# Cross-attention and routed FFN on one core: where the scatters wait, and how the last layer norm is shared between engines

## The chip, the cores and the metric

One core of a Trainium2 chip runs the whole program. The metric is the device time of one execution in microseconds (us). Three runs of the kernel before took 785.79, 787.87 and 788.98 us; the median is 787.87 us.

## The reference, cut to what matters

```python
x = x + attention(_layernorm(x), ctx)              # x: 4096 tokens x 256, 32 tiles of 128 tokens
# FFN on h = _layernorm(x):
scores = softmax(h @ wg)                           # 8 experts
gates, idx = top_k(scores, 2)                      # each token goes to two experts
disp[e] = rows of h sent to expert e               # room for 1280 rows per expert
y[e] = silu(disp[e] @ fc1[e].T + b1[e]) @ fc2[e] + b2[e]
res = h + sum over the token's two experts of gate * y
ffn = (res - mean(res)) * rsqrt(var(res) + 1e-5) * gamma + beta
out = x + ffn
```

The part "h + sum of gate * y" and everything behind it is what the change touches. A token appears once in the rows of one expert and can appear again in those of another.

## The kernel before, in words

The program has three stages. Attention and the router run first, token tile by token tile; they leave `x` after attention in the SBUF tile `X` and store each normalised row twice in HBM: in `xn_rows`, from which the experts gather, and in `sum_rows`, in which the result `res` is built.

**Expert stage.** Eight experts have room for 1280 rows each, cut into five steps of 256 rows (`SPE` = 5), so there are 40 steps `st` of two halves (`NST` = 40). TensorE does fc1 of step c and fc2 of step c-1 (line 1082); steps beyond an expert's token count are reduced to a few matmuls. Each fp32 product is three matmuls of split operands (lines 763 to 765). VectorE adds the bias and writes `y_sb` (line 1443), of which there are two, for even and odd steps; before it overwrites one it waits for the scatters of step st-2, which read it (line 1440). ScalarE multiplies by the gate (line 712). GpSimd's queue then adds each half of 128 rows to `sum_rows` with an indirect DMA that accumulates (line 522). GpSimd goes through this by hand-written order (lines 541 to 546): gather of step st+4, scatter of step st-2, then one add of `beta` to a tile of `X`. Before each step's scatters it waits until both scatters of the step before have landed (line 519):

```python
u = st % 2
wait(pool, scattered[1 - u], 32 * ((st + 1) // 2))
for q in range(2):
    pool.wait_ge(sem("y_scaled"), 2 * st + q + 1)
```

**Last stage.** SyncE's queue waits for all scatters (lines 361, 362), loads `sum_rows` back into `res` in nine pieces (line 366), and stores the output two tiles at a time in the order of the tiles (line 369). The 32 tiles are taken in eight quads. All engines are ordered by semaphores counted over quads, and every engine's order is written out in its own loop:

- ScalarE (lines 733 to 754): for the first tile of quad k+2 it computes the mean (line 738), its negative (741) and the variance (743); for quad k it computes all four tiles of z = res * rstd + nmr (line 753).
- VectorE (lines 1480 to 1512), in turn k: `bn_stats` of three tiles of quad k (1484); nmr = -mean * rstd of quad k-1 (1488); three `bn_aggr` (1493); small operations for variance + eps and -mean (1496 to 1499), the last of which releases GpSimd; z * gamma of the quad k-2 for one or two tiles (1504); z + X of quad k-3 as two operations of two tiles each (1511), each of which releases a store.
- GpSimd (lines 551 to 560): rstd = (variance + eps)^-0.5 of quad k (555), then z * gamma of three or two tiles of quad k-1 (560; `on_pool`, line 201).

## Time and profile before

| what | value |
|---|---|
| median of three runs | 787.87 us |
| the profiled execution | 790.12 us, of which its span is 788.4 us |
| attention and router | to 317.8 us of the span |
| expert stage, from the first transpose to the last matmul | 317.8 to about 737 us |
| last scatter, then the last stage | to 746.4 us, then to 788.4 us |
| TensorE, VectorE, ScalarE, GpSimd busy | 87%, 73%, 50%, 53% of the span |
| last addition on VectorE ends | 785.3 us (784.12 + 1.20) |
| store of two tiles, issue to landing | 2.3 us median |
| one of the loads of expert weights by SyncE (line 359, 1 MB), issue | at 483.17 us |

The profile is of one execution, and 1.7 us of its time lie outside the span. Times in it count from the start of the span. A row "A B ..." of a timeline or a chain gives start and duration. An instruction's duration holds its fill and drain; of merged rows (x2, x3) the next start minus the start tells what one more of them costs.

### The profile page before, as it was taken

What the parts mean: (1) busy time and instruction counts of PE and PEld (TensorE: products, weight loads), DVE (VectorE), ACT (ScalarE), POOL (GpSimd) and SP (SyncE); (2) the same over time, 40 slices, a digit from 0 to 9 for tenths busy, and PEclk for the clock granted to TensorE, in tenths of its full rate; (3) what the DMA queues carried; (4) which work ended last, traced back from release to release, by engine and by line L of the source; (5) the groups of instructions that cost most, each with busy time, mean ns of one, the idle gap of its engine ahead of it and who ended that gap; (6) DMA issues with size and microseconds to landing.
All of it is one profiled execution on the core that took longest, in us unless ns stands there. A gap on an engine that the chain in (4) does not pass through costs nothing.

```text
span 788.4 us, 15743 instructions
## 1 busy us (share of the span) xinstructions
PE 687.2 (87%) x5636; PEld 653.1 (83%) x5636; DVE 573.2 (73%) x1221; ACT 396.4 (50%) x903; POOL 416.4 (53%) x468
## 2 busy tenths in 40 slices
PE   4799999999999934799999998999999999999300
PEld 3589999999999813799999997999999999999300
DVE  4679898997887787656556669887597566845088
ACT  2245555655655533445445557455474455634084
POOL 5835465465454210724554557868567553732466
PEclk9689999999999955799999999999999999999755
DMA  9401010110110140423433545445455342421474
GB/s 282 163 15 39 30 42 28 42 42 28 42 42 27 42 139 4 147 51 62 108 73 66 109 108 109 99 89 108 99 111 122 54 92 48 64 33 16 61 242 164
DMA packets 55332, 63.85 MB, mean 81 GB/s; under 512 B 9296, under 2 KB 50512, under 8 KB 55120
## 3 DMA queue, kind: packets, MB, share of 16 engines
q0 software_dynamic: 15360, 21.31, 16.7%
q1 hardware_dynamic: 34784, 40.96, 16.0%
q8 instruction: 56, 0.92, 0.5%
q10 hardware_dynamic: 5104, 0.44, 0.5%
q14 instruction: 28, 0.23, 0.1%
HBM read 38.96 MB, written 23.72 MB: 80 GB/s over the span
## 4 chain that ended last, share of the span: by engine, by line
PE 79%; DVE 9%; DMA 6%; issue 3%; POOL 1%; ACT 1%; SPq 0%; DVEq 0%; POOLq 0%; ACTq 0%
PE banks L763 17%; PE banks L765 17%; PE banks L764 17%; PE banks L876 8%; PE banks L862 6%; PE banks L850 5%; DMA sum_rows<-y_sb,slot_ids 4%; PE banks L1003 2%; PE banks L937 2%; DVE oh_lo L1403 1%; DVE z L1511 1%; DMA wq_sb<-in_wqT 1%; PE banks L793 1%; PE banks L889 1%; PE banks L924 1%
## 5 line engine op out<-in xcount | busy, mean ns | idle before, releaser
L522 POOL DMA_INDIRECT sum_rows<-y_sb,slot_ids x80 | 130.1, 1627 | 165.3 <-ACT y_sb L712 131.0
L722 ACT ACTIVATE hraw<-banks,b_now 128x256 f32<-128x256 f32 x320 | 132.6, 477 | 92.0 <-PE banks L765 89.4
L763 PE MATMUL banks<-xT_hi,w_hi 128*128 128x256 f32 x560 | 161.0, 288 | 0.0
L765 PE MATMUL banks<-xT_hi,w_lo 128*128 128x256 f32 x560 | 158.1, 282 | 0.0
L764 PE MATMUL banks<-xT_lo,w_hi 128*128 128x256 f32 x560 | 158.0, 282 | 0.0
L763 PE MATMUL banks<-w_hi,h_hi 128*128 128x256 f32 x528 | 148.8, 282 | 2.2 <-DVE y_sb L1443 1.2
L764 PE MATMUL banks<-w_lo,h_hi 128*128 128x256 f32 x528 | 148.6, 281 | 0.0
L765 PE MATMUL banks<-w_hi,h_lo 128*128 128x256 f32 x528 | 148.4, 281 | 0.0
L1457 DVE TENSOR_TENSOR h_lo<-hraw,h_hi 128x512 fp32r<-128x512 f32 x160 | 116.2, 726 | 5.5
L511 POOL DMA_INDIRECT xg<-xn_rows,slot_ids x80 | 89.9, 1123 | 52.6 <-DVE slot_ids L1419 33.1
L1455 DVE CAST h_hi<-hraw 128x512 fp32r<-128x512 f32 x160 | 78.8, 493 | 46.7 <-ACT hraw L722 46.1
L763 PEld LDWEIGHTS banks<-xT_hi,w_hi 128*128 128x128 f32 x560 | 106.0, 189 | 0.0
L764 PEld LDWEIGHTS banks<-xT_lo,w_hi 128*128 128x128 f32 x560 | 106.0, 189 | 0.0
L765 PEld LDWEIGHTS banks<-xT_hi,w_lo 128*128 128x128 f32 x560 | 105.9, 189 | 0.0
L763 PEld LDWEIGHTS banks<-w_hi,h_hi 128*128 128x128 f32 x528 | 99.4, 188 | 2.8 <-issue 2.8
L627 ACT ACTIVATE probsT<-banks 124x384 f32<-124x384 f32 (+1 forms) x128 | 56.0, 437 | 87.2 <-PE banks L862 87.0
L764 PEld LDWEIGHTS banks<-w_lo,h_hi 128*128 128x128 f32 x528 | 99.4, 188 | 0.0
L765 PEld LDWEIGHTS banks<-w_hi,h_lo 128*128 128x128 f32 x528 | 99.4, 188 | 0.0
L876 PE MATMUL banks<-VB,probsT 124*128 124x51 f32 (+2 forms) x640 | 86.0, 266 | 0.0
L876 PEld LDWEIGHTS banks<-VB,probsT 124*128 124x128 f32 x640 | 83.3, 193 | 0.0
L689 ACT ACTIVATE xT_hi<-banks 128x512 fp32r<-128x512 f32 x40 | 24.1, 602 | 113.0 <-PE banks L1003 113.0
L487 POOL TENSOR_TENSOR rstd<-var,minus_half 128x1 f32<-128x1 f32 x32 | 17.4, 545 | 118.5 <-DVE var L1323 118.5
(188 smaller groups left out, 1425.9 us busy)
## 6 DMA issues: line engine op xcount, KB each, us to landing
w1raw<-in_w1T SPq DMA_DIRECT2D x8, 1024.0 KB, 6.7
w2raw<-in_w SPq DMA_DIRECT2D x8, 1024.0 KB
xn_rows<-xn SPq DMA_DIRECT2D x32, 128.0 KB, 1.7
sum_rows<-xn SPq DMA_DIRECT2D x32, 128.0 KB, 1.8
out<-z SPq DMA_DIRECT2D x16, 256.0 KB, 2.3
res<-sum_rows SPq DMA_DIRECT2D x7, 512.0 KB, 8.5
X<-in_x SPq DMA_DIRECT2D x2, 1280.0 KB, 13.3
xg<-xn_rows,slot_ids POOLq DMA_INDIRECT x80, 4.3
```

Source lines behind the costliest of these rows:

```text
L511: g.indirect_dma_start(xg[:, st % XR, q, :], None, xn_rows, bass.IndirectOffsetOnAxis(ap=slot_ids[:, st, 0, q:q + 1], axis=0), bounds_chec ...
L522: g.indirect_dma_start(sum_rows, bass.IndirectOffsetOnAxis(ap=slot_ids[:, st, 1, q:q + 1], axis=0), y_sb[:, u, q, :], None, bounds_check=N ...
L627: a.activation(probsT[:, j0:j0 + w, :].rearrange("r j q -> r (j q)"), banks[0:JW, PT, 0:w * P], ACT.Copy).then_inc(sem("pT_made"), 1)
L722: a.activation(hraw[:, j // 2, j % 2, :], banks[:, j // 2, (j % 2) * 256:(j % 2 + 1) * 256], ACT.Silu, bias=b1_now[:, (c // SPE) % 2, j:j ...
L763: t_.matmul(o, a_hi, b_hi, start=first, stop=False)
L764: t_.matmul(o, a_hi, b_lo, start=False, stop=False)
L765: return t_.matmul(o, a_lo, b_hi, start=False, stop=last)
L850: m = t_.matmul(banks[:, 2 * f + h, 0:KC], qq[rows, f, qs], kk[rows, ds((2 * b + f) * KH + h * KC, KC)], start=(n == 0), stop=(n == 2))
L862: m = t_.transpose(banks[0:JW, PT, (j - j0) * P:(j - j0 + 1) * P], probs[:, 1 - u, f * KH + j * JS:f * KH + j * JS + JW], ident[:])
L876: m = t_.matmul(banks[:, PV, f * VW + a_:f * VW + a_ + n_], probsT[:, NJ * f + j, :], VB[:, ds(((2 * b + f) * NJ + j) * VW + a_, n_)], sta ...
L1455: v.tensor_copy(hi, raw).then_inc(sem("h_hi_made"), 1)
L1457: v.tensor_tensor(lo, raw, hi.bitcast(f32), ALU.subtract).then_inc(sem("h_lo_made"), 1)
```

## The change

Two things are changed. GpSimd waits for the scatters of the step before only at the first step of each expert. In the last stage each quad is shared out anew: ScalarE does the statistics and the normalisation of tiles 0 and 1 and GpSimd multiplies these by gamma; VectorE alone does tiles 2 and 3, with `bn_stats`, `bn_aggr` and two fused operations of two tensors and a per-row scalar, (res - mean) * gamma and then z * rstd + X. VectorE adds `X` to the first two tiles as before. The stores follow the order in which the halves of the quads are made.

```diff
--- before.py
+++ after.py
@@ -191,16 +191,20 @@
         RES_LOADS = [(0, 2), (2, 4)] + [(QT * k, QT * (k + 1)) for k in range(1, NQ)]
         res = sb("res", [P, NT, D], f32, C)
         z = sb("z", [P, NT, D], f32, C)
-        unused = sb("unused", [P, 2, D], f32, C)
+        unused, squares = sb("unused", [P, 2, D], f32, C), sb("squares", [P, 2, D], f32, C)
         st_d, mv_d = sb("st_d", [P, NT, 6], f32, C), sb("mv_d", [P, NT, 2], f32, C)
         m16_d, nmu_d, var_d, vare_d, rstd_d, nmr_d = (sb(n, [P, NT], f32, C)
                                                       for n in ("m16_d", "nmu_d", "var_d", "vare_d", "rstd_d", "nmr_d"))
         eps_d, zero_d = sb("eps_d", [P, QT], f32, C), sb("zero_d", [P, QT], f32, C)
         C.close()
 
-        def on_pool(k):
-
-            return 3 if k % 2 == 0 else 2
+        def halves_in_order():
+
+            for k in range(1, NQ + 2):
+                if k <= NQ:
+                    yield QT * (k - 1) + 2
+                if k >= 2:
+                    yield QT * (k - 2)
 
         banks = root.enter_context(nc.psum_tensor("banks", [P, 8, 512], f32))
         PT, PV, TR, PJ = 4, 5, 6, 7
@@ -364,9 +368,9 @@
 
             for n, (a, b) in enumerate(RES_LOADS):
                 sp.dma_start(res[:, a:b, :], sum_t[:, a:b, :]).then_inc(load_res[n], 16)
-            for g in range(NT // 2):
+            for g, a in enumerate(halves_in_order()):
                 sp.wait_ge(sem("out_made"), g + 1)
-                sp.dma_start(out_t[:, 2 * g:2 * g + 2, :], z[:, 2 * g:2 * g + 2, :]).then_inc(stored, 16)
+                sp.dma_start(out_t[:, a:a + 2, :], z[:, a:a + 2, :]).then_inc(stored, 16)
             sp.wait_ge(stored, 16 * (NT // 2))
 
 
@@ -516,7 +520,8 @@
 
                 if within(st, NST):
                     u = st % 2
-                    wait(pool, scattered[1 - u], 32 * ((st + 1) // 2))
+                    if st % SPE == 0:
+                        wait(pool, scattered[1 - u], 32 * ((st + 1) // 2))
                     for q in range(2):
                         pool.wait_ge(sem("y_scaled"), 2 * st + q + 1)
                         g.indirect_dma_start(sum_rows, bass.IndirectOffsetOnAxis(ap=slot_ids[:, st, 1, q:q + 1], axis=0),
@@ -555,8 +560,8 @@
                     g.tensor_tensor(rstd_d[:, quad], vare_d[:, quad], minus_half[:, 0:QT], ALU.pow)\
                         .then_inc(sem("rstd3_made"), 1)
                 if k >= 1:
-                    for t in range(QT * (k - 1), QT * (k - 1) + on_pool(k - 1)):
-                        pool.wait_ge(sem("z_made"), t + 1)
+                    for t in (QT * (k - 1), QT * (k - 1) + 1):
+                        pool.wait_ge(sem("z_made"), 2 * (k - 1) + t % QT + 1)
                         g.tensor_tensor(z[:, t, :], z[:, t, :], gamma_sb[:], ALU.mult).then_inc(sem("z_scaled"), 1)
 
 
@@ -730,26 +735,28 @@
             expert_steps(act, expert_step)
 
 
-            def first_of_quad(k):
+            def first_two(k):
 
                 if k < NQ:
-                    t = QT * k
-                    res_loaded(act, t)
-                    a.activation(unused[:, 0, :], res[:, t, :], ACT.Copy, scale=1.0 / (16 * D),
-                                 accum_out=m16_d[:, t:t + 1]).then_inc(sem("mean16_made"), 1)
-                    act.wait_ge(sem("mean16_made"), k + 1)
-                    a.activation(nmu_d[:, t:t + 1], m16_d[:, t:t + 1], ACT.Copy, scale=-16.0)\
+                    a0 = QT * k
+                    for t in (a0, a0 + 1):
+                        res_loaded(act, t)
+                        a.activation(unused[:, t % 2, :], res[:, t, :], ACT.Copy, scale=1.0 / (16 * D),
+                                     accum_out=m16_d[:, t:t + 1]).then_inc(sem("mean16_made"), 1)
+                    act.wait_ge(sem("mean16_made"), 2 * (k + 1))
+                    a.activation(nmu_d[:, a0:a0 + 2], m16_d[:, a0:a0 + 2], ACT.Copy, scale=-16.0)\
                         .then_inc(sem("act_stats_made"), 1)
-                    a.activation(unused[:, 1, :], res[:, t, :], ACT.Square, scale=-1.0 / 16, bias=m16_d[:, t:t + 1],
-                                 accum_out=var_d[:, t:t + 1]).then_inc(sem("act_stats_made"), 1)
-
-            first_of_quad(0)
-            first_of_quad(1)
+                    for t in (a0, a0 + 1):
+                        a.activation(squares[:, t % 2, :], res[:, t, :], ACT.Square, scale=-1.0 / 16,
+                                     bias=m16_d[:, t:t + 1], accum_out=var_d[:, t:t + 1])\
+                            .then_inc(sem("act_stats_made"), 1)
+
+            first_two(0)
+            first_two(1)
             for k in range(NQ):
-                first_of_quad(k + 2)
+                first_two(k + 2)
                 act.wait_ge(sem("nmr_made"), k + 1)
-                for t in range(QT * k, QT * (k + 1)):
-                    res_loaded(act, t)
+                for t in (QT * k, QT * k + 1):
                     a.activation(z[:, t, :], res[:, t, :], ACT.Identity, scale=rstd_d[:, t:t + 1],
                                  bias=nmr_d[:, t:t + 1]).then_inc(sem("z_made"), 1)
 
@@ -1473,43 +1480,40 @@
 
             dve.wait_ge(sem("beta_added"), NT)
 
-            def wide(row_tile, n):
-                return row_tile[:].unsqueeze(1).to_broadcast([P, n, D])
-
             dve.wait_ge(sem("tail_consts"), 2)
-            for k in range(NQ + 3):
+            for k in range(NQ + 2):
+                first, last = slice(QT * k, QT * k + 2), slice(QT * k + 2, QT * (k + 1))
                 if k < NQ:
-                    for t in range(QT * k + 1, QT * (k + 1)):
+                    for t in range(last.start, last.stop):
                         res_loaded(dve, t)
                         v.bn_stats(st_d[:, t, :], res[:, t, :]).then_inc(sem("st3_made"), 1)
                 if 1 <= k <= NQ:
-                    quad = slice(QT * (k - 1), QT * k)
+                    two = slice(QT * (k - 1), QT * (k - 1) + 2)
                     dve.wait_ge(sem("rstd3_made"), k)
-                    v.tensor_tensor(nmr_d[:, quad], nmu_d[:, quad], rstd_d[:, quad], ALU.mult)\
+                    v.tensor_tensor(nmr_d[:, two], nmu_d[:, two], rstd_d[:, two], ALU.mult)\
                         .then_inc(sem("nmr_made"), 1)
                 if k < NQ:
-                    dve.wait_ge(sem("st3_made"), 3 * (k + 1))
-                    for t in range(QT * k + 1, QT * (k + 1)):
+                    dve.wait_ge(sem("st3_made"), 2 * (k + 1))
+                    for t in range(last.start, last.stop):
                         v.bn_aggr(mv_d[:, t, :], st_d[:, t, :]).then_inc(sem("mv3_made"), 1)
-                    dve.wait_ge(sem("mv3_made"), 3 * (k + 1))
-                    three = slice(QT * k + 1, QT * (k + 1))
-                    v.tensor_tensor(vare_d[:, three], mv_d[:, three, 1], eps_d[:, 1:QT], ALU.add)
-                    v.tensor_tensor(nmu_d[:, three], zero_d[:, 1:QT], mv_d[:, three, 0], ALU.subtract)
-                    dve.wait_ge(sem("act_stats_made"), 2 * (k + 1))
-                    v.tensor_tensor(vare_d[:, QT * k:QT * k + 1], var_d[:, QT * k:QT * k + 1], eps_d[:, 0:1], ALU.add)\
+                    dve.wait_ge(sem("mv3_made"), 2 * (k + 1))
+                    v.tensor_tensor(vare_d[:, last], mv_d[:, last, 1], eps_d[:, 0:2], ALU.add)
+                    dve.wait_ge(sem("act_stats_made"), 3 * (k + 1))
+                    v.tensor_tensor(vare_d[:, first], var_d[:, first], eps_d[:, 0:2], ALU.add)\
                         .then_inc(sem("var3_made"), 1)
-                if 2 <= k <= NQ + 1:
-                    a, b = QT * (k - 2) + on_pool(k - 2), QT * (k - 1)
-                    dve.wait_ge(sem("z_made"), b)
-                    v.tensor_tensor(z[:, a:b, :], z[:, a:b, :], wide(gamma_sb, b - a), ALU.mult)\
-                        .then_inc(sem("z_scaled_dve"), 1)
-                if k >= 3:
-                    for a in (QT * (k - 3), QT * (k - 3) + 2):
-                        pooled = sum(on_pool(n) for n in range(k - 3)) + min(on_pool(k - 3), a + 2 - QT * (k - 3))
-                        dve.wait_ge(sem("z_scaled"), pooled)
-                        dve.wait_ge(sem("z_scaled_dve"), k - 2)
-                        v.tensor_tensor(z[:, a:a + 2, :], z[:, a:a + 2, :], X[:, a:a + 2, :], ALU.add)\
-                            .then_inc(sem("out_made"), 1)
+                    for t in range(last.start, last.stop):
+                        v.scalar_tensor_tensor(z[:, t, :], res[:, t, :], mv_d[:, t, 0:1], gamma_sb[:],
+                                               ALU.subtract, ALU.mult).then_inc(sem("z_scaled_dve"), 1)
+                if 1 <= k <= NQ:
+                    dve.wait_ge(sem("z_scaled_dve"), 2 * k)
+                    for t in range(QT * (k - 1) + 2, QT * k):
+                        m = v.scalar_tensor_tensor(z[:, t, :], z[:, t, :], rstd_d[:, t:t + 1], X[:, t, :],
+                                                   ALU.mult, ALU.add)
+                    m.then_inc(sem("out_made"), 1)
+                if k >= 2:
+                    two = slice(QT * (k - 2), QT * (k - 2) + 2)
+                    dve.wait_ge(sem("z_scaled"), 2 * (k - 1))
+                    v.tensor_tensor(z[:, two, :], z[:, two, :], X[:, two, :], ALU.add).then_inc(sem("out_made"), 1)
 
 
 _OUT_SHAPE = (4, 1024, 256)
```

## Rows read from the trace of the kernel before

**Rows 1.** Page, part 4: the whole chain that ended last, by line.

```profile
PE banks L763 17%; PE banks L765 17%; PE banks L764 17%; PE banks L876 8%; PE banks L862 6%; PE banks L850 5%; DMA sum_rows<-y_sb,slot_ids 4%; PE banks L1003 2%; PE banks L937 2%; DVE oh_lo L1403 1%; DVE z L1511 1%; DMA wq_sb<-in_wqT 1%; PE banks L793 1%; PE banks L889 1%; PE banks L924 1%
```

**Rows 2.** Waits, 320 to 746 us: us in total, times, longest.

```profile
POOL sum_rows L522 <- DMA sum_rows<-y_sb,slot_ids: 18.2, 6, 3.1
...
DVE y_sb L1443 <- DMA sum_rows<-y_sb,slot_ids: 2.8, 2, 1.4
...
PE banks L763 <- DVE y_sb L1443: 1.2, 1, 1.2
```

**Rows 3.** Timeline of GpSimd, 726 to 744 us: start, duration, idle before.

```profile
727.83 1.55 POOL L522 DMA_INDIRECT sum_rows<-y_sb,slot_ids  x1 [7.97 <-ACT y_sb L712]
...
734.29 1.55 POOL L522 DMA_INDIRECT sum_rows<-y_sb,slot_ids  x1 [3.05 <-DMA sum_rows<-y_sb,slot_ids]
...
740.72 1.57 POOL L522 DMA_INDIRECT sum_rows<-y_sb,slot_ids  x1 [3.01 <-DMA sum_rows<-y_sb,slot_ids]
742.59 1.56 POOL L522 DMA_INDIRECT sum_rows<-y_sb,slot_ids  x1 [0.30 <-issue]
```

**Rows 4.** Timeline of ScalarE, 724 to 745 us.

```profile
726.50 0.90 ACT L712 ACTIVATE y_sb<-y_sb,xg 128x256 f32<-128x256 f32 x2
...
737.55 0.51 ACT L712 ACTIVATE y_sb<-y_sb,xg 128x256 f32<-128x256 f32 x1 [2.26 <-DVE y_sb L1443]
```

**Rows 5.** Chain, two scatters from issue to landing: start, us.

```profile
483.70 7.55 DMA sum_rows<-y_sb,slot_ids
...
742.59 3.81 DMA sum_rows<-y_sb,slot_ids
```

**Rows 6.** Chain, one turn of VectorE's loop in the last stage, and its last additions.

```profile
763.42 0.99 DVE st_d L1484 x3
764.41 0.31 DVE nmr_d L1488
764.72 0.23 DVE mv_d L1493 x3
...
765.54 0.33 DVE z L1504
765.88 1.20 DVE z L1511 x2
767.08 0.99 DVE st_d L1484 x3
...
784.12 1.20 DVE z L1511 x2
```

**Rows 7.** Timeline of ScalarE, 757 to 763 us.

```profile
758.14 0.40 ACT L738 ACTIVATE unused<-res 128x256 f32<-128x256 f32 x1
...
759.27 2.06 ACT L753 ACTIVATE z<-res,nmr_d,rstd_d 128x256 f32<-128x256 f32 x4
```

**Rows 8.** VectorE's fused operations in the attention stage: groups by form, then timeline.

```profile
L1132 DVE SCALAR_TENSOR_TENSOR q_lo<-banks,bq_sb,q_hi 128x256 fp32r<-128x256 f32 x32 | 14.0, 479 | 12.3 <-ACT q_hi L593 12.3
...
L1279 DVE TENSOR_TENSOR valsT_lo<-banks,valsT_hi 128x256 fp32r<-128x256 f32 x32 | 13.3, 414 | 0.7 <-ACT valsT_hi L639 0.7
...
102.56 0.88 DVE L1132 SCALAR_TENSOR_TENSOR q_lo<-banks,bq_sb,q_hi 128x256 fp32r<-128x256 f32 x2
```

**Rows 9.** Timeline of VectorE, 744 to 789 us.

```profile
753.62 1.08 DVE L1484 BATCH_NORM_STATS2 st_d<-res 128x6 f32<-128x256 f32 x3 [1.66 <-DMA res<-sum_rows]
...
776.09 0.15 DVE L1499 TENSOR_TENSOR vare_d<-var_d,eps_d 128x1 f32<-128x1 f32 x1
...
778.90 2.35 DVE L1511 TENSOR_TENSOR z<-z,X 128x512 f32<-128x512 f32 x2
```

**Rows 10.** Timeline of GpSimd, 744 to 789 us.

```profile
756.84 2.09 POOL L560 TENSOR_TENSOR z<-z,gamma_sb 128x256 f32<-128x256 f32 x3 [0.36 <-ACT z L753]
...
776.32 1.39 POOL L555 TENSOR_TENSOR rstd_d<-vare_d,minus_half 128x4 f32<-128x4 f32 x1 [0.66 <-DVE vare_d L1499]
777.68 5.29 POOL L560 TENSOR_TENSOR z<-z,gamma_sb 128x256 f32<-128x256 f32 x5
```

## What I predict, and from which rows

> **What bounds the kernel now.** I read the chain that ended last first. TensorE holds most of it, and the matmuls of lines 763 to 765 alone are 51% of the span; scatters into `sum_rows` are 4%, the additions of line 1511 are 1% [rows 1]. So the change works at the edges of a kernel that TensorE bounds, and each part has to be read in its own stretch: the waits of the expert stage, the timelines just before its end, and one turn of VectorE's loop in the last stage.
>
> In the expert stage GpSimd waited six times for an earlier scatter, 18.2 us in all, but only what reaches TensorE or the end counts. VectorE waited 2.8 us for scatters before overwriting `y_sb`, and TensorE passed on 1.2 us of that, once [rows 2]. The rest of the 18.2 us is hidden behind TensorE until TensorE is finished. From there the scatters are the path: the last step's first scatter starts at 740.72, released by a landing and not by ScalarE, which had scaled the last half at 737.55 + 0.51 = 738.06 [rows 3, 4]. The last scatter starts at 742.59 and lands 3.81 us later, at 746.40 [rows 3, 5]. SyncE loads `res` right behind that.
>
> In the last stage, from 746.4 to 788.4 us, VectorE has no gap in the steady turns: from one group of `bn_stats` to the next are 767.08 - 763.42 = 3.66 us [rows 6]. ScalarE needs 759.27 - 758.14 = 1.13 us for the statistics of one tile and 2.06 / 4 = 0.52 us for each normalised tile, 3.2 us a turn [rows 7]. VectorE bounds the stage, by half a microsecond.
>
> **Part 1, the scatters at the end.** Removed are the waits before steps 36 to 39 (the last expert's steps 1 to 4). The last step's second half is ready at 738.06. The way from ScalarE to a scatter's start is 727.83 - (726.50 + 0.90) = 0.43 us [rows 3, 4]. The queue is free: step 38's two scatters start no later than now (first at 734.29, and one more takes 742.59 - 740.72 = 1.87 us), so GpSimd is done with them and with the last step's first half before 738.5. The last scatter then starts at 738.5 in place of 742.59, **4.1 us earlier**, and with the same 3.81 us lands at 742.3. VectorE's own wait on `y_sb` stays; it asks for step 37, which landed before step 38's scatter could start. What is late next is TensorE itself, so no more than this is to be had. The bound on the other side: up to four scatters can now be in the queue together. The slowest landing in the chain took 7.55 us [rows 5], beside a weight load issued 0.5 us ahead of it, at 483.17; with it 0.4 us would be left of the 4.1. I take 3.81, since no weights are loaded at the end.
>
> **Part 2, the scatters in the middle.** The one scatter that held TensorE up started at 483.70 and took 7.55 us [rows 5]. Steps with few tokens run short there and GpSimd falls behind; without the waits its scatters start up to about 1.4 us earlier, bound again by gathers that stand between them. I take **1.0 us** of TensorE's 1.2, with 0 and 1.4 (VectorE's longest such wait, [rows 2]) as ends.
>
> **Part 3, a turn of VectorE.** Removed: one `bn_stats` of three, 0.99 / 3 = 0.33; one `bn_aggr`, 0.08; one small operation of 0.15 at most [rows 9]; the gamma product, 0.33 for one tile and 0.60 for two in turns, 0.47 in the mean; one addition of two, 0.60 [rows 6]. That is 1.6 us. Added: four fused operations on 128x256. The trace of before has none with both tensors in SBUF. Nearest is line 1132, also fp32 with a per-row scalar, one input in PSUM: 479 ns, and a second one behind it costs 0.88 - 0.48 = 0.40 us; the plain operation of that size takes 414 ns [rows 8] and 0.33 us a piece [rows 6]. I take 0.40, so 1.6 us; the lower end is 0.33, so 1.3 us. **The fused form saves almost nothing in VectorE's steady turn**: 0.66 + 0.31 + about 0.45 for `bn_aggr` and small operations + 1.60 + 0.60 = 3.62 us, against 3.66.
>
> The waits inside a turn: the second pair of fused operations works on the quad before, whose rstd GpSimd made a turn ago, and whose first pair was finished a turn ago. So no wait for a neighbour's pipeline is new. ScalarE has 2 x 1.13 + 2 x 0.52 = 3.3 us (less one small operation), still under 3.6. GpSimd has one power and two products in place of two or three.
>
> **Part 4, the first turns.** ScalarE now does two tiles of statistics before VectorE can release the power. Quad 1 arrives at 753.62 [rows 9]; ScalarE is ready at 755.9, and I put V(1), the start of VectorE's last small operation of quad 1, at 756.0. That is some 0.7 us later than in the old order, where 1.13 us sufficed. V(2) follows after 3.62 - 0.60 (no addition yet): 759.0. Five more turns give V(7) = 759.0 + 5 x 3.62 = 777.1; before it was 776.09 [rows 9]. So the steady part loses 1.0 us.
>
> **Part 5, the last turns.** Here lies the gain. Before, the end comes 788.4 - 776.09 = 12.3 us after V(7): two more quads wait for their additions, and four of them run in a row behind GpSimd's five products. After: four fused operations and an addition, 2.2 us; nmr, 0.3; ScalarE's two tiles by V + 3.6; GpSimd's two products at 0.70 us each in the clear (2.09 / 3) or 1.06 beside VectorE (5.29 / 5) [rows 10], so by V + 4.6 to V + 5.3; with the handovers the last addition ends at V + 5.8. From the last addition's end, 784.12 + 1.20 = 785.32 [rows 6], to the end of the span are 3.1 us, and this stays. V(7) + 8.9 = 786.0, so the last stage is 2.4 us shorter.
> Ends: at 0.33 us for a fused operation V(2) is 758.7, the turn 3.34 and the end 784.3, a gain of 4.1. The other end is the next paragraph's.
>
> **Contention.** At 778.90 two additions took 2.35 us, where two take 1.20 otherwise, while GpSimd's five products ran at 1.06 us in place of 0.70 [rows 6, 9, 10]: they took turns, and VectorE lost some 0.55 us to each product. In the steady turns of before this hardly shows, because GpSimd's products fall beside `bn_stats`. After the change VectorE has five operations with two SBUF inputs per turn where it had 2 to 3, about 2.2 us of 3.6. GpSimd's power ends about 1.6 us behind V (0.24 to start and 1.39, [rows 10]), while the products may meet the additions and only then `bn_stats`. At one such meeting per turn, six turns cost 3.3 us: V(7) = 780.4, end 789.3, a loss of 0.9.
> The Trainium skill (SBUF — State Buffer, "Who interferes with whom") says that a VectorE instruction with two SBUF inputs contends with a GpSimd instruction that reads SBUF, and that the first to issue holds the port for its whole length. It speaks against this change and would give the 789.3; the rows at 778.90 agree with it.
>
> **Sum.** 4.1 + 1.0 + 2.4 = 7.5 us. Against the profiled execution that makes 790.12 - 7.5 = 782.6; the median of the runs lies 2.25 us under it, and 787.87 - 7.5 = **780.4 us**.
>
> **Rivals.**
> 1. Taking turns at the port in every steady turn, as worked out: 4.1 + 1.0 - 0.9 = 4.2 us gained, 783.7. For it: the rows at 778.90. Against it: two thirds of GpSimd's work can still lie beside `bn_stats` and the power. 0.18, two thirds of it still over the bound below.
> 2. The scatters land no sooner: four at once stretch each other, the last takes up to 7.55 us, and 0.4 + 1.0 + 2.4 = 3.8 us are gained, 784.1. The change would then not do what it says, since the waiting only moves into the DMA. For it: the 7.55. Against it: that one had a weight load beside it, and pairs of scatters 1.87 us apart land in 3.81. 0.06.
> 3. Slower: GpSimd's power blocks VectorE too. It now starts when the first fused operation starts. If its 1.39 us and two products at 0.55 us were all lost to VectorE in seven turns, that is 7 x 2.5 = 17 us, and 787.87 - 7.5 + 17 = 797.5. It decides from a loss of 1.6 us a turn. Against it: at 776.32 the power ran beside additions that kept their 0.6 us. 0.03.
> 4. Better: fused operations at 0.33 us, and a clean end: 4.1 + 1.4 + 4.1 = 9.6 us, 778.3. 0.09.
>
> **How the numbers follow.** The forecast has 0.64. A measurement of this kernel can tell about 0.5%, 3.9 us, from no change. Faster by more: 0.64 + 0.12 + 0.09 = 0.85; within: 0.06 + 0.06 = 0.12; slower: 0.03. The range takes in rival 4 and the faster ends at the bottom, with a microsecond for the spread of runs, and rivals 1 and 2 at the top: 777.0 to 784.3.
>
> **What would show it.** The last scatter starts near 738.5 and lands in under 4.5 us; no wait of GpSimd for a scatter within an expert; fused operations of 0.48 us, pitch 0.40; VectorE's turn 3.6 us, or over 4 if rival 1 holds, with fused operations or additions of over 0.8 us; V(7) to the end 8.9 us in place of 12.3. The prediction is wrong if the turn shrinks to 3.3 or grows to 4.2, if the loads of `res` start later than 4 us before the old time, or if TensorE's stretch from 317.8 on changes by more than 2 us.

## The result, and the profile after

The changed kernel takes 784.03 us (median of 20 runs, 780.12 to 786.59), against 787.84 us of the kernel before in 20 runs beside it: 3.8 us less. The ratio is 0.9956, with a 95% interval of 0.9942 to 0.9969. I had forecast 7.5 us less, so **the direction was right and the size was twice too large**. The profiled execution took 785.25 us, of which 783.5 are its span (790.12 and 788.4 before).

The page's chain by line, in which the scatters have gone from 4% to 1% of the span [rows 1]:

```profile
PE banks L770 18%; PE banks L772 18%; PE banks L771 18%; PE banks L883 8%; PE banks L869 6%; PE banks L857 5%; PE banks L1010 2%; PE banks L944 2%; DMA sum_rows<-y_sb,slot_ids 1%; DVE oh_lo L1410 1%; DMA wq_sb<-in_wqT 1%; PE banks L896 1%; PE banks L800 1%; PE banks L931 1%; DVE oh_id L1405 1%
```

Waits of the expert stage, 317 to 746 us (us in total, times, longest):

```profile
POOL sum_rows L527 <- ACT y_sb L717: 148.7, 33, 15.6
...
DVE y_sb L1450 <- DMA sum_rows<-y_sb,slot_ids: 1.8, 2, 1.1
...
PE banks L770 <- DVE y_sb L1450: 0.6, 1, 0.6
```

GpSimd has no entry for an earlier scatter any more (18.2 us before, [rows 2]); it waits for ScalarE. VectorE still waits 1.8 us for scatters, 2.8 before, and TensorE passes on 0.6 us of it, 1.2 before. The end of the stage, from GpSimd's timeline, the chain and SyncE's timeline:

```profile
738.10 1.56 POOL L527 DMA_INDIRECT sum_rows<-y_sb,slot_ids  x1 [1.20 <-ACT y_sb L717]
...
738.10 3.70 DMA sum_rows<-y_sb,slot_ids
741.87 0.37 SPq L370
```

The last scatter is released by ScalarE, starts at 738.10, lands at 741.80 and the loads of `res` start at 741.87, where the kernel before stood at 742.59, 746.40 and 746.47 [rows 3, 5]. VectorE's last `y_sb` is at 736.37 in this execution and was at 737.10, so 0.7 us of the 4.6 come from further ahead, and 3.9 us from the end itself.

**So the stage of the layer norm gained nothing**: from the first load's issue to the end it lasts 783.5 - 741.87 = 41.6 us, where it was 788.4 - 746.47 = 41.9. Even these 0.3 us come from the loads: quad 1 reached the engines 5.9 us behind the first load's issue in this execution and 7.15 us behind it in that of before. Counted from the arrival of quad 1 the stage takes 783.5 - 747.77 = 35.7 us, where it took 788.4 - 753.62 = 34.8 [rows 9]. First ScalarE's row at that arrival, then one steady turn of VectorE's loop:

```profile
747.77 0.42 ACT L744 ACTIVATE unused<-res 128x256 f32<-128x256 f32 x1 [1.10 <-DMA res<-sum_rows]
```

```profile
767.63 0.74 DVE L1489 BATCH_NORM_STATS2 st_d<-res 128x6 f32<-128x256 f32 x2
768.29 0.70 DVE L1493 TENSOR_TENSOR nmr_d<-nmu_d,rstd_d 128x2 f32<-128x2 f32 x1
...
769.34 0.87 DVE L1505 SCALAR_TENSOR_TENSOR z<-res,mv_d,gamma_sb 128x256 f32<-128x256 f32 x2
770.12 0.87 DVE L1510 SCALAR_TENSOR_TENSOR z<-z,rstd_d,X 128x256 f32<-128x256 f32 x2
770.92 0.68 DVE L1516 TENSOR_TENSOR z<-z,X 128x512 f32<-128x512 f32 x1
771.52 0.74 DVE L1489 BATCH_NORM_STATS2 st_d<-res 128x6 f32<-128x256 f32 x2
```

The turn is 771.52 - 767.63 = 3.89 us (3.66 before, [rows 6]; 3.62 predicted). The fused operations cost 0.87 for two, 0.40 for one more, as taken from line 1132. What is out of line is nmr, two columns wide: 0.70 us. The single operations around it, of GpSimd and VectorE:

```profile
766.76 1.53 POOL L565 TENSOR_TENSOR z<-z,gamma_sb 128x256 f32<-128x256 f32 x1
...
767.02 0.68 DVE L1516 TENSOR_TENSOR z<-z,X 128x512 f32<-128x512 f32 x1
...
768.26 0.72 POOL L565 TENSOR_TENSOR z<-z,gamma_sb 128x256 f32<-128x256 f32 x1
768.29 0.70 DVE L1493 TENSOR_TENSOR nmr_d<-nmu_d,rstd_d 128x2 f32<-128x2 f32 x1
...
769.50 1.18 POOL L560 TENSOR_TENSOR rstd_d<-vare_d,minus_half 128x4 f32<-128x4 f32 x1 [0.52 <-DVE vare_d L1502]
```

GpSimd's first product by gamma is issued at 766.76 and takes 1.53 us where 0.72 us is the length of the second. It ends at 768.29, so its own 0.72 us began at about 767.6, just when VectorE's addition was through. It then runs beside `bn_stats`, and the second product, 768.26 to 768.98, lies exactly over nmr, which is done at the same moment. The last turns:

```profile
773.15 0.15 DVE L1502 TENSOR_TENSOR vare_d<-var_d,eps_d 128x2 f32<-128x2 f32 x1
...
775.41 0.69 DVE L1493 TENSOR_TENSOR nmr_d<-nmu_d,rstd_d 128x2 f32<-128x2 f32 x1
...
777.51 1.20 DVE L1516 TENSOR_TENSOR z<-z,X 128x512 f32<-128x512 f32 x1 [0.62 <-POOL z L565]
779.33 0.69 DVE L1516 TENSOR_TENSOR z<-z,X 128x512 f32<-128x512 f32 x1 [0.62 <-POOL z L565]
...
774.54 4.75 POOL L565 TENSOR_TENSOR z<-z,gamma_sb 128x256 f32<-128x256 f32 x4
```

Four products take 4.75 us, 1.19 each; VectorE waits 0.62 us for them twice, and its first addition there takes 1.20 us in place of 0.68. From the start of the last small operation (773.15) to the end of the span are 10.35 us: 12.3 before, 8.9 predicted.

### The profile page after: what moved, and what is told of

The parts are those of the page before. It is cut to its first block, busy times and chain, and to the rows that moved or that the text cites. A ratio compares the mean times of both kernels' runs of the same rounds, so it can differ in the third digit from the quotient of the medians.

```text
span 783.5 us, 15691 instructions
## 1 busy us (share of the span) xinstructions
PE 687.7 (88%) x5636; PEld 653.4 (83%) x5636; DVE 571.1 (73%) x1213; ACT 395.3 (50%) x919; POOL 411.9 (53%) x464
## 4 chain that ended last, share of the span: by engine, by line
PE 82%; DVE 8%; DMA 3%; POOL 2%; issue 2%; ACT 1%; SPq 0%; POOLq 0%; DVEq 0%; ACTq 0%
PE banks L770 18%; PE banks L772 18%; PE banks L771 18%; PE banks L883 8%; PE banks L869 6%; PE banks L857 5%; PE banks L1010 2%; PE banks L944 2%; DMA sum_rows<-y_sb,slot_ids 1%; DVE oh_lo L1410 1%; DMA wq_sb<-in_wqT 1%; PE banks L896 1%; PE banks L800 1%; PE banks L931 1%; DVE oh_id L1405 1%
## 5 line engine op out<-in xcount | busy, mean ns | idle before, releaser
L1464 DVE TENSOR_TENSOR h_lo<-hraw,h_hi 128x512 fp32r<-128x512 f32 x160 | 114.1, 713 | 5.5
L515 POOL DMA_INDIRECT xg<-xn_rows,slot_ids x80 | 85.6, 1070 | 52.6 <-DVE slot_ids L1426 33.1
```

The costliest lines, as they stand in the source:

```text
L515: g.indirect_dma_start(xg[:, st % XR, q, :], None, xn_rows, bass.IndirectOffsetOnAxis(ap=slot_ids[:, st, 0, q:q + 1], axis=0), bounds_chec ...
L1464: v.tensor_tensor(lo, raw, hi.bitcast(f32), ALU.subtract).then_inc(sem("h_lo_made"), 1)
```

## The experiments

Every kernel was timed beside the kernel before. "Stage" is the time from the issue of the first load of `res` to the end of the span, in the profiled execution; "end" the part of it from the start of the last quad's last small operation on; "from quad 1" the part from the moment when quad 1 has arrived and the first engine starts on it; "turn" is VectorE's in the steady part. Quad 1 arrives 5.5 to 7.2 us behind the first load's issue, which differs from execution to execution; counted from quad 1 the changed kernel's two executions agree to within 0.1 us.

| kernel | ratio to before, 95% interval | stage | from quad 1 | turn | end |
|---|---|---|---|---|---|
| before | | 41.9 | 34.8 | 3.66 | 12.3 |
| after | 0.9956, 0.9942 to 0.9969 | 41.6 | 35.7 | 3.89 | 10.35 |
| after, timed again | 0.9966, 0.9949 to 0.9983 | 41.7 | 35.7 | 3.90 | 10.4 |
| scatter part alone | 0.9947, 0.9928 to 0.9967 | 41.1 | 34.9 | 3.66 | 12.3 |
| last stage alone | 1.0005, 0.9991 to 1.0020 | 42.2 | 35.7 | 3.90 | 10.4 |
| no products on GpSimd | 0.9880, 0.9859 to 0.9901 | 35.5 | 29.3 | 3.39 | 7.4 |
| nmr before the addition | 0.9950, 0.9932 to 0.9967 | 40.8 | 35.3 | 4.07 | 9.5 |
| nmr on ScalarE | 0.9946, 0.9921 to 0.9970 | 40.9 | 34.4 | 3.55 | 10.0 |
| gamma in PSUM | 0.9957, 0.9934 to 0.9979 | 42.5 | 36.5 | 4.41 | 10.3 |
| gamma and the intermediate in PSUM | 0.9922, 0.9897 to 0.9948 | 40.0 | 33.6 | 3.54 | 10.0 |
| old stage, gamma in PSUM | 0.9931, 0.9904 to 0.9957 | 40.7 | 34.3 | 3.38 and 4.18 in turns | 11.5 |
| last quad on VectorE too | 0.9924, 0.9900 to 0.9949 | 37.6 | 31.7 | 3.54 | 8.1 |
| and nmr on ScalarE | 0.9911, 0.9883 to 0.9939 | 37.5 | 31.1 | 3.51 | 8.6 |

The ratios are of whole executions, whose first 740 us scatter by some microseconds from run to run, so stages and turns are compared in the profiles and the ratios only where their intervals part.

### The two parts by themselves

The first takes only the scatter part, the second only the new last stage:

```diff
                     u = st % 2
-                    wait(pool, scattered[1 - u], 32 * ((st + 1) // 2))
+                    if st % SPE == 0:
+                        wait(pool, scattered[1 - u], 32 * ((st + 1) // 2))
```

> The scatter part alone, with the last stage of before. If the parts are independent, as the spans of the two profiles suggest (last landing 746.40 before, 741.80 after), the last scatter lands at about 742, the last stage lasts 42 us as before, and the time is 4.4 us under the kernel before (ratio 0.9945). Rival: the earlier start of the loads only moves a wait into the last stage; then the stage is 43 us or longer and the gain under 3 us.

> The new last stage alone, with the waits between scatters of before. If the new sharing is a wash, as the profile after shows (41.6 us from the first load's issue to the end against 41.9), the time is 0 to 0.5 us under the kernel before (ratio 0.9995). Rival, my prediction's sum: 2.4 us under it (ratio 0.997), and the profile after was then an unlucky one.

Measured: 0.9947 and 1.0005. All of the gain is the scatters'; the last stage alone gives none, and the interval leaves room for a loss of 1.6 us or a gain of 0.7. The rival with my prediction's sum, 0.997, lies outside it. First the scatter part (GpSimd, SyncE, then VectorE at the arrival of quad 1), then the last stage alone (SyncE, then VectorE at that arrival and in a turn):

```profile
737.98 1.56 POOL L523 DMA_INDIRECT sum_rows<-y_sb,slot_ids  x1 [1.20 <-ACT y_sb L713]
...
741.80 7.89 SPq L366 DMA_DIRECT2D res<-sum_rows  x9
...
747.96 1.08 DVE L1485 BATCH_NORM_STATS2 st_d<-res 128x6 f32<-128x256 f32 x3 [1.22 <-DMA res<-sum_rows]
```

```profile
744.66 8.10 SPq L370 DMA_DIRECT2D res<-sum_rows  x9
...
751.21 0.75 DVE L1488 BATCH_NORM_STATS2 st_d<-res 128x6 f32<-128x256 f32 x2 [0.68 <-DMA res<-sum_rows]
...
771.00 0.74 DVE L1488 BATCH_NORM_STATS2 st_d<-res 128x6 f32<-128x256 f32 x2
771.66 0.71 DVE L1492 TENSOR_TENSOR nmr_d<-nmu_d,rstd_d 128x2 f32<-128x2 f32 x1
...
774.90 0.74 DVE L1488 BATCH_NORM_STATS2 st_d<-res 128x6 f32<-128x256 f32 x2
```

With the scatter part the way from VectorE's last `y_sb` to the first load is 741.80 - 736.26 = 5.5 us, in the changed kernel 741.87 - 736.37 = 5.5; without it, in the last stage alone, 744.66 - 735.36 = 9.3, as before (746.47 - 737.10 = 9.4). That is 3.8 to 3.9 us in both pairs. The new stage keeps its turn of 3.9 us and its nmr of 0.7 us whatever the scatters do. The rival (a wait moved into the last stage) falls: the stage of the first kernel is 41.1 us, not 43. From quad 1 on the old stage takes 34.8 and 34.9 us and the new one 35.7 us three times, so in the profiles the new sharing costs 0.8 to 0.9 us; the intervals of the ratios are too wide to show that.

### Without GpSimd's products

```diff
-                        pool.wait_ge(sem("z_made"), 2 * (k - 1) + t % QT + 1)
-                        g.tensor_tensor(z[:, t, :], z[:, t, :], gamma_sb[:], ALU.mult).then_inc(sem("z_scaled"), 1)
...
-                    dve.wait_ge(sem("z_scaled"), 2 * (k - 1))
+                    dve.wait_ge(sem("z_made"), 2 * (k - 1))
```

> The changed kernel without GpSimd's product by gamma for tiles 0 and 1 of each quad; VectorE's addition waits for ScalarE instead. That part of the computation is left out. Theory port: VectorE's small product nmr (line 1493, 0.70 us in each steady turn) is held up by GpSimd's second product, so without it nmr falls to 0.14, the turn from 3.89 to 3.3 to 3.4 us, five turns give 2.5 us and the last turns another 2 us: the last stage lasts about 37 us. Rival pipeline: nmr waits for the bn_stats ahead of it or for rstd, whatever GpSimd does; then the turn stays at 3.8 to 3.9 and only the end is shorter, by about 2 us.

The start of one turn of VectorE, and of the next:

```profile
765.68 0.74 DVE L1488 BATCH_NORM_STATS2 st_d<-res 128x6 f32<-128x256 f32 x2
766.34 0.14 DVE L1492 TENSOR_TENSOR nmr_d<-nmu_d,rstd_d 128x2 f32<-128x2 f32 x1
...
769.07 0.74 DVE L1488 BATCH_NORM_STATS2 st_d<-res 128x6 f32<-128x256 f32 x2
```

This kernel leaves a part of the computation out, so it is a measurement and no candidate. nmr takes 0.14 us and the turn 3.39 us, as expected; the stage falls by 6.1 us to 35.5, more than to the 37 expected. The five turns from the last small operation of quad 2 to that of quad 7 take 770.21 - 753.23 = 17.0 us in place of 20.4, which is 0.5 us a turn and another 1.0 us in the first, and the end is 10.35 - 7.4 = 3.0 us shorter; the loads came 0.3 us later. **The turn of 3.89 us is 3.39 us of VectorE's own work and one collision of 0.5 us with a product.** VectorE's own work without collisions is thus less than the 3.62 us that I had summed, and the collision more. The rival, that nmr waits for the pipeline or for rstd, is refuted.

### Moving nmr

nmr of quad k ahead of the addition of turn k, and in another kernel on ScalarE:

```diff
+                if k < NQ:
+                    dve.wait_ge(sem("rstd3_made"), k + 1)
+                    v.tensor_tensor(nmr_d[:, first], nmu_d[:, first], rstd_d[:, first], ALU.mult)\
+                        .then_inc(sem("nmr_made"), 1)
                 if k >= 2:
```

```diff
-                act.wait_ge(sem("nmr_made"), k + 1)
+                act.wait_ge(sem("rstd3_made"), k + 1)
+                act.wait_ge(sem("act_stats_made"), 3 * (k + 1))
+                for t in (QT * k, QT * k + 1):
+                    a.activation(nmr_d[:, t:t + 1], nmu_d[:, t:t + 1], ACT.Copy, scale=rstd_d[:, t:t + 1])\
+                        .then_inc(sem("nmr_made"), 1)
+                act.wait_ge(sem("nmr_made"), 2 * (k + 1))
```

> The changed kernel with nmr of quad k computed in turn k, just ahead of the addition, while GpSimd's power has just ended and no product of it has begun. Theory port: nmr costs 0.12 there; VectorE's next operation with two SBUF inputs after the addition is the small addition of eps (line 1500), which may meet the second product for 0.1 to 0.3 us; turn 3.4 to 3.7 us, last stage 1 to 3 us shorter than 41.6, the time 5 to 7 us under the kernel before. Rival pipeline: nmr costs 0.6 us wherever it stands; turn 3.9, nothing gained.

> The changed kernel with nmr computed by ScalarE, as two products of one column each, just before its normalisation. Theory sum of the port: in one turn VectorE's operations with two SBUF inputs (four fused at 0.40, one addition at 0.60, three small ones at 0.08) and GpSimd's two products (0.70 each) add up to 3.8 us, and the turn is 3.89; taking 0.08 away from that sum gives a turn of 3.7 to 3.8 us, and the collision only moves to the small addition of eps. Rival, nmr was the one operation in the way: turn 3.3 to 3.5 us, last stage over 2 us shorter than 41.6.

First nmr ahead of the addition, then nmr on ScalarE (there the operations between two groups of `bn_stats`):

```profile
768.27 0.94 POOL L565 TENSOR_TENSOR z<-z,gamma_sb 128x256 f32<-128x256 f32 x1
768.54 0.69 DVE L1512 TENSOR_TENSOR nmr_d<-nmu_d,rstd_d 128x2 f32<-128x2 f32 x1
...
769.15 0.68 DVE L1517 TENSOR_TENSOR z<-z,X 128x512 f32<-128x512 f32 x1
769.17 1.24 POOL L565 TENSOR_TENSOR z<-z,gamma_sb 128x256 f32<-128x256 f32 x1
```

```profile
765.96 0.74 DVE L1494 BATCH_NORM_STATS2 st_d<-res 128x6 f32<-128x256 f32 x2
766.80 0.25 DVE L1500 BATCH_NORM_AGGREGATE mv_d<-st_d 128x2 f32<-128x6 f32 x2
767.09 0.24 DVE L1502 TENSOR_TENSOR vare_d<-mv_d,eps_d 128x2 f32<-128x2 f32 x1
...
769.51 0.74 DVE L1494 BATCH_NORM_STATS2 st_d<-res 128x6 f32<-128x256 f32 x2
```

My expectation for the first was wrong: nmr still takes 0.69 us, since here the first product is issued 0.27 us ahead of it, and the turn grew to 4.07 us where I expected 3.4 to 3.7. The stage is 0.8 us shorter than in the changed kernel all the same (0.4 from quad 1 on), through its end of 9.5 us. It also left the place where it had filled VectorE's wait between `bn_stats` and `bn_aggr`. For the second the rival was nearer: I expected 3.7 to 3.8 us, the turn is 3.55, just outside the rival's 3.3 to 3.5; but the stage is only 0.7 us shorter (1.3 from quad 1 on), where the rival had over 2, since three longer turns of 4.40, 3.95 and 3.81 us come first. One collision is left, with the small addition of eps (0.24 us in place of 0.16), because ScalarE is later with its tiles and the products now run beside `bn_stats`. The sum of what uses the port, on which I had built that expectation, is no measure of the turn.

### Taking operands off SBUF

If a collision needs two SBUF inputs on VectorE, then an operand in PSUM takes it away. First only gamma lies in PSUM; then the result of the first fused operation too; then the old stage with gamma in PSUM for its products on VectorE:

```diff
+            gamma_ps = banks[:, 7, 0:D]
+            v.tensor_copy(gamma_ps, gamma_sb[:]).then_inc(sem("gamma_copied"), 1)
+            dve.wait_ge(sem("gamma_copied"), 1)
...
-                        v.scalar_tensor_tensor(z[:, t, :], res[:, t, :], mv_d[:, t, 0:1], gamma_sb[:],
+                        v.scalar_tensor_tensor(z[:, t, :], res[:, t, :], mv_d[:, t, 0:1], gamma_ps,
```

```diff
+            def scaled(t):
+                return banks[:, (t // QT) % 2, (t % 2) * D:(t % 2 + 1) * D]
...
-                        v.scalar_tensor_tensor(z[:, t, :], res[:, t, :], mv_d[:, t, 0:1], gamma_ps,
+                        v.scalar_tensor_tensor(scaled(t), res[:, t, :], mv_d[:, t, 0:1], gamma_ps,
...
-                        m = v.scalar_tensor_tensor(z[:, t, :], z[:, t, :], rstd_d[:, t:t + 1], X[:, t, :],
+                        m = v.scalar_tensor_tensor(z[:, t, :], scaled(t), rstd_d[:, t:t + 1], X[:, t, :],
```

```diff
+            for n in range(2):
+                v.tensor_copy(banks[:, 7, n * D:(n + 1) * D], gamma_sb[:]).then_inc(sem("gamma_copied"), 1)
+            dve.wait_ge(sem("gamma_copied"), 2)
...
-                return row_tile[:].unsqueeze(1).to_broadcast([P, n, D])
+                return banks[:, 7, 0:n * D].rearrange("p (n d) -> p n d", d=D)
```

> The changed kernel with a copy of gamma in PSUM for the first pair of fused operations, so that they have one SBUF input; the same operations on every engine. Theory sum of the port: the sum falls by 2 x 0.40 to 3.0 us, below VectorE's own 3.39 us of a turn without products; turn 3.4 to 3.6 us, last stage 2 to 3.5 us shorter than 41.6. Rival, what slows VectorE is not its second SBUF input but GpSimd at work as such: turn 3.9 us.

> As before it, and the result of the first fused operation is kept in PSUM too, so that none of the four has two SBUF inputs. Theory sum of the port: 0.60 + 0.24 + 1.40 = 2.2 us, turn 3.39 us as without products, or up to 3.5 where a product still meets the addition; products 0.7 to 0.8 us each; last stage 37.5 to 38.5 us, time 7 to 8 us under the kernel before (ratio 0.990 to 0.991). Rival: turn 3.9 us as in the changed kernel, or fused operations that PSUM makes slower than 0.48 us.

> The scatter part with the last stage of before, whose products by gamma on VectorE read gamma from PSUM. Theory sum of the port, asked of the old stage: its turn of 3.66 us was the sum of 0.47 + 1.20 + 0.25 on VectorE and 2.5 x 0.70 on GpSimd = 3.67; without 0.47 the port no longer binds, and the turn falls to VectorE's own 3.25 to 3.45 us, the last stage by 1.5 to 2.5 us. Rival, the old turn was VectorE's own work: 3.66 stays.

Gamma alone in PSUM, single operations of GpSimd and VectorE:

```profile
772.93 1.01 POOL L560 TENSOR_TENSOR rstd_d<-vare_d,minus_half 128x4 f32<-128x4 f32 x1 [1.84 <-DVE vare_d L1505]
...
773.90 0.72 POOL L565 TENSOR_TENSOR z<-z,gamma_sb 128x256 f32<-128x256 f32 x1
773.94 0.96 DVE L1513 SCALAR_TENSOR_TENSOR z<-z,rstd_d,X 128x256 f32<-128x256 f32 x1
...
774.59 0.91 POOL L565 TENSOR_TENSOR z<-z,gamma_sb 128x256 f32<-128x256 f32 x1
774.83 1.21 DVE L1519 TENSOR_TENSOR z<-z,X 128x512 f32<-128x512 f32 x1
```

This was a miss, and the most telling one. The first fused pair is free now, and with it the power, which takes 1.01 us where it took 1.18: it had been held up as well. But so the products start 0.17 us earlier against VectorE's order, in front of the second fused operation (0.96 us in place of 0.48) and of the addition (1.21 in place of 0.68). **Two full collisions a turn, 4.41 - 3.39 = 1.0 us, though fewer operations compete for the port than before.** That is outside my 3.4 to 3.6 and outside the rival's 3.9 us. Both intermediate operands in PSUM, one turn:

```profile
766.42 0.73 POOL L565 TENSOR_TENSOR z<-z,gamma_sb 128x256 f32<-128x256 f32 x1
766.46 0.48 DVE L1517 SCALAR_TENSOR_TENSOR z<-banks,rstd_d,X 128x256 f32<-128x256 f32 x1
...
766.85 0.84 DVE L1523 TENSOR_TENSOR z<-z,X 128x512 f32<-128x512 f32 x1
...
767.10 1.18 POOL L565 TENSOR_TENSOR z<-z,gamma_sb 128x256 f32<-128x256 f32 x1
```

At the very same phase the fused operation beside the first product, 0.48 us, is not touched: it reads one tensor from PSUM. So GpSimd at work as such, the rival of the kernel before, does not slow VectorE. The addition loses 0.16 us. The turn is 3.54 us (3.39 to 3.5 expected), nmr 0.14, and the stage 40.0 us, not the 37.5 to 38.5 that I expected: the end stayed at 10.0 us. In the old stage gamma in PSUM gave turns of 3.38 and 4.18 us, because now the additions meet a product in every second turn:

```profile
762.42 1.07 DVE L1489 BATCH_NORM_STATS2 st_d<-res 128x6 f32<-128x256 f32 x3
...
764.86 1.82 DVE L1516 TENSOR_TENSOR z<-z,X 128x512 f32<-128x512 f32 x2
766.60 1.07 DVE L1489 BATCH_NORM_STATS2 st_d<-res 128x6 f32<-128x256 f32 x3
...
768.78 1.28 DVE L1516 TENSOR_TENSOR z<-z,X 128x512 f32<-128x512 f32 x2
769.98 1.07 DVE L1489 BATCH_NORM_STATS2 st_d<-res 128x6 f32<-128x256 f32 x3
```

The mean of the two, 3.78 us, is no better than 3.66, and the stage is 0.4 us shorter than with the scatter part alone (40.7 and 41.1 us), not 1.5 to 2.5. The expectation drawn from the sum of the port fell here a third time.

### The end, and a version that beats both

The last quad's tiles 0 and 1 are made by VectorE too, with the mean that ScalarE has computed; ScalarE and GpSimd stop one quad earlier, and the last two stores change places. Then nmr goes to ScalarE as above.

```diff
+                if k == NQ - 1:
+                    for t in range(first.start, first.stop):
+                        v.scalar_tensor_tensor(scaled(t), res[:, t, :], nmu_d[:, t:t + 1], gamma_ps,
+                                               ALU.add, ALU.mult).then_inc(sem("z_scaled_dve"), 1)
...
+                if k == NQ:
+                    dve.wait_ge(sem("z_scaled_dve"), 2 * NQ + 2)
+                    for t in range(QT * (k - 1), QT * (k - 1) + 2):
+                        m = v.scalar_tensor_tensor(z[:, t, :], scaled(t), rstd_d[:, t:t + 1], X[:, t, :],
+                                                   ALU.mult, ALU.add)
+                    m.then_inc(sem("out_made"), 1)
```

> Fused operations through PSUM, and the last quad's tiles 0 and 1 made by VectorE too, with four more fused operations in place of nmr, ScalarE's two normalisations, GpSimd's two products and an addition. Theory: at the end VectorE waits for GpSimd's products of the last two quads (10.0 us from the last power's release to the end of the span, against 7.4 without any products). With the last quad on VectorE these are 1.6 + 0.8 + 0.6 + 1.6 + 0.6 = 5.2 us of its own, up to 0.5 for one collision and 3.2 for the last store: 8.6 to 9.0, so the last stage is 38.6 to 39.2 us long (40.0 with the fused operations through PSUM alone). Rival: the end is set by collisions and stores whatever engine does the work, and 10 us stay.

> The kernel before this one, and nmr computed by ScalarE. If what counts in a turn is VectorE's own work plus the collisions left, nmr's 0.12 us go but the gap it filled between bn_stats and bn_aggr opens (0.18 us in two earlier runs): turn 3.3 to 3.55 us, no gain over the kernel before this one beyond 0.5 us. Rival: nmr on VectorE was worth 0.3 us or more a turn, 2 us in all.

> The changed kernel again, on the chip of the two kernels above: 0.995 to 0.997 of the kernel before; turn 3.89 us, with the 0.70 us of nmr, and 10.4 us from the last release to the end, if these belong to the kernel and not to one execution.

VectorE at the end, the last quad on VectorE, from its last small operation on:

```profile
769.98 0.15 DVE L1514 TENSOR_TENSOR vare_d<-var_d,eps_d 128x2 f32<-128x2 f32 x1
770.05 0.88 DVE L1517 SCALAR_TENSOR_TENSOR banks<-res,mv_d,banks 128x256 f32<-128x256 f32 x2
...
774.63 0.68 DVE L1538 TENSOR_TENSOR z<-z,X 128x512 f32<-128x512 f32 x1
```

From 769.98 to the end of the span at 778.1 are 8.1 us, better than the 8.6 to 9.0 expected: only 0.06 us of the additions' time is lost to a product, and from the end of the last addition (774.63 + 0.68) to the end of the span are 2.8 us and not 3.2. The stage is 2.4 us shorter than with gamma and the intermediate in PSUM, of which 1.9 us are the end and 0.5 an earlier arrival of quad 1. The ratios of these two kernels, 0.9922 and 0.9924, do not show this gain; it stands in the profiles alone. With nmr on ScalarE the turn is 3.51 us and the stage 37.5 (0.6 us less counted from quad 1), so hardly a gain over the one before, as expected. That kernel takes 779.27 us where the changed kernel, on the same chip, takes 785.23: 0.9911 against 0.9966 of the kernel before, with intervals that do not meet. Its lead over the kernel without nmr on ScalarE (0.9924) is within the intervals.

The changed kernel timed again gives 0.9966, turns of 3.90 us with an nmr of 0.71 or 0.72, and 10.4 us at the end. These belong to the kernel, not to one execution.

## Why the prediction was right or wrong

**Part 1, the scatters at the end: right.** I had 4.1 us, the pairs above show 3.8 to 3.9. The last scatter starts 0.76 us after ScalarE's last scaling (738.10 - 736.83 - 0.51), not 0.43, which is the 0.3 us that are missing. I had misread the row of before: 726.50 with 0.90 us is two scalings, and the scatter of 727.83 waited only for the first of them, which takes 0.51 us [rows 4], so the way was 727.83 - 727.01 = 0.82 us there too. The last scatter lands in 3.70 us. Rival 2 did not come, but four scatters at once were not put to the test: GpSimd's last six start at 727.04, 728.89, 730.75, 732.61, 735.32 and 738.10 and land in 3.7 to 3.9 us, so two were under way at a time and hardly ever three.

**Part 2, the middle: mis-sized.** I took 1.0 us. TensorE's wait behind `y_sb` fell from 1.2 to 0.6, and is 0.7 in the kernel with the scatter part alone and 1.0 with the last stage alone, so some 0.3 to 0.6 us are gained, read from the waits of single executions. TensorE's stretch, from the first transpose to the start of the last matmul, agrees: 736.05 - 317.56 = 418.5 us, where it was 736.78 - 317.83 = 419.0. A load of weights still lies beside the scatter in question, which takes 7.6 us as before.

**Part 3, the turn: wrong, and this is the step that failed.** I summed 3.62 us, put the meetings with GpSimd's products at nothing in the forecast, and took 0.31 us for nmr from a row in which it already stood beside a product. The cost of a fused operation, 0.40 us, was right. VectorE's own work is 3.39 us, but nmr costs 0.63 us in each turn because GpSimd's second product is pushed onto it. My argument that four fused operations and the addition make the products meet them was right in the mechanism and wrong in the place: these five run behind one another undisturbed, GpSimd waits 0.8 us for them, and the bill comes at the first two-input operation after `bn_stats`. A turn of 3.89 in place of 3.62 is 0.27 us, and the first steady turn, 4.86 us, another 1.2 us: in all 20.4 us from V(2) to V(7) against my 18.1. The old turn read the same way had collisions too: in [rows 6] nmr costs 0.31 in place of 0.12, and the small addition behind it takes 0.43 us in that turn and 0.16 in one without a product beside it. So my remark that contention hardly shows in the steady turns of before was wrong too. Without these meetings its turns are, by my estimate from these rows, about 3.2 and, with two tiles for gamma, 3.5, in the mean 3.3 us; no run leaves the products out of the old stage. **So the new sharing left VectorE's own work about where it was, 3.3 (estimated) and 3.4 us (measured), and made the collisions dearer, 0.3 and 0.5 us.**

**Part 4, the first turns: wrong by 1.6 us, in the kernel's favour, and mostly by luck.** V(2) is 752.73 - 741.87 = 10.9 us behind the first load, I had 12.5. Of the difference 1.2 us are luck: quad 1 arrived 5.9 us behind the first load, where I took the 7.15 us of the execution before, and in the other kernels it was 5.5 to 6.6. The other 0.4 us are work that I put too high: V(1) follows 2.2 us behind the arrival and V(2) 2.8 us behind V(1), where I had 2.4 and 3.0; no product runs in that turn yet. This hid part of the error of part 3.

**Part 5, the last turns: right in direction, 1.45 us off.** The end is 10.35 us and not 8.9. The products of the last two quads take 1.19 us each, more than the 1.06 that I took as the worst, and the addition that waits for them costs 1.20 us. Without products it is 7.4 us.

**The sum.** The stage's end is 2.0 us shorter (12.3 to 10.35) and the way to it 1.7 us longer, 0.3 us in all; without the 1.2 us by which quad 1 came sooner the stage would have lost 0.9 us. 3.9 at the end of the expert stage, 0.3 from the last stage, and what the middle gives: 4 to 5 us in the spans, 3.8 us in the medians. Rival 1, taking turns at the port in every turn, comes nearest to what happened: one meeting with a product in every steady turn, some 0.5 us each. Its sign was a turn over 4 us with fused operations or additions over 0.8 us, though, and the turn was 3.89, the meeting fell on nmr, and VectorE's own work was 3.39 us and not 3.62. That it gave 783.7 us where 784.03 were measured is partly luck: it had too much for the middle and for the turns, too little for the last turns (8.9 for 10.35 us), and did not know of the sooner quad 1. None of my own signs for being wrong came either (a turn of 3.3 or 4.2 us, loads later than 4 us before the old time, TensorE's stretch changed by 2 us), so they were set too wide. I gave rival 1 0.18, on the ground that two thirds of GpSimd's work could lie beside `bn_stats` and the power; the products did move there, but one of them reached beyond. It should have been the likeliest case, because the rows of before showed the cost of a meeting, 0.55 us, and nothing in the order kept the products away. The Trainium skill (SBUF — State Buffer, "Who interferes with whom") had the collision right, and the runs agree on which operations take part: 0.48 us with one input in PSUM, 0.96 with both in SBUF at the same phase. By its account the order of issue decides who blocks. That fits the meetings of two operations here (the product of 768.26 against nmr of 768.29), but it was not enough where a third one held the port: in the changed kernel a product issued at 766.76, while the second fused operation was running, was overtaken by the addition of 767.02.

What is not settled is who gets the port when a product is already waiting. In the changed kernel the addition passes it; ahead of the addition, nmr, which had a wait for rstd in front of it, did not (768.27 against 768.54); with gamma in PSUM the addition of 774.83 did not pass the product of 774.59 either. A handover in the order of requests, made ahead of the start, would fit the first two, not the third, and is only argued.

## What to carry to other kernels

Before an engine pair that shares a port is given more two-input work, take the phase into account, not the sum: read from single operations which one of VectorE's two-input operations a GpSimd operation meets, and price each meeting at what is left of the GpSimd operation (here up to 0.55 us), also for an operation that is two columns wide. An operand moved to PSUM, if TensorE has left it free, takes an operation out of this and costs that operation nothing; but it also moves the phase, and with gamma alone in PSUM the turn grew. And let the last items of a pipeline over several engines be finished by the engine that ends last anyway: 1.9 us of 40 in the profile here.

## What the runs showed of the hardware that I had not expected

- A VectorE operation of two columns took 0.14 us or 0.70 us, by whether a GpSimd product of 0.72 us was running (768.26 and 768.29), and GpSimd's power on 128x4 took 1.01 or 1.18 us by whether the VectorE operations that it started beside had one or two SBUF inputs.
- Making one engine faster made the stage slower: gamma in PSUM brought the power's end 0.17 us forward and the turn from 3.89 to 4.41 us.
- A product that waits for the port can be held for 0.8 us by two VectorE operations in a row, and show 1.53 us in place of 0.72.
- A fused operation with a per-row scalar costs the same with its inputs in SBUF or one of them in PSUM (477 and 475 ns, each the median of 16), and the same with its result in PSUM (0.87 or 0.88 us for two).
